# A graph kernel with groups of 64 nodes in place of 128, and rows of g spread to edges in three bf16 parts

## What is computed

```python
h = relu(layernorm(x))
x = x + gcn(h)          # D^-1/2 A D^-1/2 h W, relu; rows of edges' dst are summed into src
h = relu(layernorm(x))
msg_fwd  = concat(h[src], edge_attr) @ W_fwd  + b_fwd     # summed into dst
msg_back = concat(h[dst], edge_attr) @ W_back + b_back    # summed into src
x = x + layernorm(leaky(mean of the messages) + h)
```

## Time and profile before

| | us |
|---|---|
| median of 3 runs (4393.7 to 4401.2) | 4395.8 |
| the profiled execution | 4403.9 |
| its span | 4402.1 |
| POOL busy (69% of the span) | 3040.5 |
| PE busy (77%) | 3390.4 |
| DVE busy (72%) | 3169.3 |
| ACT busy (42%) | 1843.2 |

### The profile page before, as it was taken

One profiled execution on the slowest core, in us unless ns is written; L12 is line 12 of the kernel. 1 busy time (PEld: TensorE's weight loads), 2 busy tenths in 40 slices (PEclk: granted clock), 3 DMA queues, 4 the chain that ended last, 5 costly groups with the idle time before them and its releaser, 6 DMA issues. The chain is left out here.

```text
span 4402.1 us, 100368 instructions
## 1 busy us (share of the span) xinstructions
PE 3390.4 (77%) x30529; PEld 2833.3 (64%) x30529; DVE 3169.3 (72%) x8051; ACT 1843.2 (42%) x4498; POOL 3040.5 (69%) x1812
## 2 busy tenths in 40 slices
PE   1454599888889888889803499889888898889945
PEld 1344587777777777777703377767767677777635
DVE  6999888888888888878614776666666666666427
ACT  1021355545555555555404144444444444444513
POOL 2666488888888888888820688778777777777210
PEclk9989899999999999999956599999999999999977
DMA  9991587777777777777786555455445555554861
GB/s 162 279 217 16 128 142 140 139 140 135 135 141 139 141 136 135 137 135 141 129 131 120 105 84 85 75 78 82 77 77 78 84 77 80 77 83 72 97 124 30
DMA packets 682054, 504.19 MB, mean 115 GB/s; under 512 B 308854, under 2 KB 593920, under 8 KB 679754
## 3 DMA queue, kind: packets, MB, share of 16 engines
q0 software_dynamic: 260032, 176.60, 36.6%
q1 hardware_dynamic: 421475, 320.75, 29.9%
HBM read 283.43 MB, written 240.12 MB: 119 GB/s over the span
## 5 line engine op out<-in xcount | busy, mean ns | idle before, releaser
L1643 POOL DMA_INDIRECT gcn_sums<-shared,ds_to_i x752 | 1309.1, 1741 | 542.5 <-ACT shared L1895 327.6
L813 POOL DMA_INDIRECT gcn_sums<-fl_sums,fl_to_i x864 | 1459.3, 1689 | 290.9 <-DMA gcn_sums<-fl_sums,fl_to_i 151.9
L1850 PE MATMUL bank<-ds_counts,ds_parts 128*128 128x256 bf16 x3675 | 605.5, 278 | 0.0
L1039 ACT COPY fl_sums<-bank 128x256 f32<-128x256 f32 x864 | 324.7, 376 | 641.8 <-DMA gcn_sums<-fl_sums,fl_to_i 303.6
L1919 ACT COPY ds_turned<-bank 128x1024 bf16<-128x1024 bf16 (+1 forms) x325 | 313.1, 963 | 613.4 <-PE bank L1835 520.7
L1883 ACT CAST ds_counts<-bank 128x392 bf16<-128x392 f32 x800 | 382.9, 490 | 225.9 <-PE bank L1794 206.4
L1870 PE MATMUL bank<-ds_turned,ds_now 128*128 128x512 bf16 (+1 forms) x1950 | 463.7, 375 | 0.0
L851 DVE SCALAR_TENSOR_TENSOR fl_same<-fl_key_b,fl_pat,from_me 128x128 f32<-128x128 bf16 x864 | 375.5, 447 | 117.0 <-PE bank L967 93.1
L1779 DVE TENSOR_TENSOR src_sums<-src_sums,bank 128x512 f32<-128x512 f32 (+1 forms) x325 | 213.2, 656 | 278.8 <-PE bank L1870 274.2
L966 PE MATMUL bank<-fl_pay,fl_same 128*128 128x128 f32 x1728 | 350.9, 285 | 66.7 <-issue 38.1
L1812 PE MATMUL bank<-shared 128*128 128x128 f32 x1504 | 306.8, 308 | 115.1 <-DVE attr_sums L1696 87.1
(11 more groups left out here) (254 smaller groups left out, 7101.6 us busy)
## 6 DMA issues: line engine op xcount, KB each, us to landing
fl_attrs<-in_edge_attr SPq DMA_DIRECT2D x108, 512.0 KB
shared<-in_edge_attr SPq DMA_DIRECT2D x186, 256.0 KB
fl_rel_b<-dst_offset SPq DMA_DIRECT2D x108, 256.0 KB
fl_key_b<-src_key SPq DMA_DIRECT2D x108, 256.0 KB
gcn_sums<-zeros SPq DMA_DIRECT2D x40, 640.0 KB
shared<-src_key SPq DMA_DIRECT2D x94, 256.0 KB
gcn_sums<-fl_sums,fl_to_i POOLq DMA_INDIRECT x864
near<-src_float SPq DMA_DIRECT2D x1, 12892.0 KB
```

The costliest lines, as they stand in the source:

```text
L813: nc.gpsimd.indirect_dma_start(out=d.tab_gcn[j % K], out_offset=bass.IndirectOffsetOnAxis(ap=to_i[:, (GPI * kk + gi) % 4, j:j + 1], axis=0 ...
L1039: nc.scalar.copy(sums[:, h, j, :], sum_bank[j % 2][:, 0:2 * F]).then_inc(staged, 1)
L1643: nc.gpsimd.indirect_dma_start(out=d.tab_gcn[j % K].rearrange("n (two f) -> (n two) f", two=2), out_offset=bass.IndirectOffsetOnAxis(ap=to ...
L1850: ins = nc.tensor.matmul(row_bank[:, 0:2 * P], parts[:, tile, s, :], counts[:, h, tile, :, :].rearrange("p b q -> p (b q)"), start=(tile = ...
```

## The change

The window has W = 64 nodes in place of 128, in both stages. `sum_hot` halves, and so do the moving side of the window sums and the addition to `attr_sums`. In `first_layer` the 64 rows of g are loaded twice, onto both halves of the partitions. They are cut into three bf16 parts that add up to the f32 value: `top` (both halves at first), then `rest` = window - top, then the upper half of `top` is overwritten by bf16(rest), `mid` is the same on the lower half, and `low` = rest - mid. `spread_hot` becomes bf16, with `part_w` counting 0 to 63 on both halves, so one product over 128 partitions adds top and mid, and a second over 64 partitions adds low. ACT makes top and mid at chunks 1 and 3 of the group before, DVE rest and low at the same chunks. The diff, cut to its core:

```diff
+W = 64
-                nc.vector.tensor_scalar(wide[:, 0:1], wide[:, 0:1], P - 0.5, None, ALU.is_gt)
+                nc.vector.tensor_scalar(wide[:, 0:1], wide[:, 0:1], W - 0.5, None, ALU.is_gt)
...
-        spread_hot = sb("spread_hot", [P, J, P])
+        spread_hot = sb("spread_hot", [P, J, P], BF16)
+        part_w = sb("part_w", [P, 1])
+        top = sb("top", [P, 2, F], BF16)
+        low = sb("low", [W, 2, F], BF16)
+        rest = sb("rest", [P, F])
+        mid = sb("mid", [W, F], BF16)
-        sum_hot = sb("sum_hot", [P, J, P])
+        sum_hot = sb("sum_hot", [P, J, W])
...
-                    sp.dma_start(window[:, h, :], d.g[bass.ds(base, P), :]).then_inc(window_in[h], 16)
+                    for cut in (slice(0, W), slice(W, P)):
+                        sp.dma_start(window[cut, h, :], d.g[bass.ds(base, W), :]).then_inc(window_in[h], 16)
...
-                nc.vector.tensor_tensor(sum_hot[:], d.iota[:].unsqueeze(1).to_broadcast([P, J, P]), rec[:, h, 2, :].unsqueeze(2).to_broadcast([P, J, P]),
+                nc.vector.tensor_tensor(sum_hot[:], d.iota[:, 0:W].unsqueeze(1).to_broadcast([P, J, W]), rec[:, h, 2, :].unsqueeze(2).to_broadcast([P, J, W]),
...
-                at = bass.ds(base, P)
-                nc.vector.tensor_tensor(d.attr_sums[:, at], d.attr_sums[:, at], win_bank[:, 0:P], ALU.add).then_inc(window_added, 1)
+                at = bass.ds(base, W)
+                nc.vector.tensor_tensor(d.attr_sums[:, at], d.attr_sums[:, at], win_bank[:, 0:W], ALU.add).then_inc(window_added, 1)
+            def window_rest(i, kk, gi):
+                g, h = group(i, kk, gi), gi % 2
+                dve.wait_ge(top_ready, 3 * g + 1)
+                dve.wait_ge(window_in[h], 32 * loads(i, kk, gi))
+                nc.vector.tensor_tensor(rest[:], window[:, h, :], top[:, h, :], ALU.subtract).then_inc(rest_ready, 1)
+            def window_low(i, kk, gi):
+                g, h = group(i, kk, gi), gi % 2
+                dve.wait_ge(top_ready, 3 * g + 3)
+                dve.wait_ge(rest_ready, g + 1)
+                at_least(dve, row_ready, 2 * (g - 1))
+                nc.vector.tensor_tensor(low[:, h, :], rest[0:W, :], mid[:], ALU.subtract).then_inc(low_ready, 1)
...
-                    nc.vector.tensor_scalar(spread_hot[:], rel_b[:, h, :, :].rearrange("p q j -> p j q"), d.part[:, 0:1], None,
+                    nc.vector.tensor_scalar(spread_hot[:], rel_b[:, h, :, :].rearrange("p q j -> p j q"), part_w[:, 0:1], None,
                                             ALU.is_equal).then_inc(spread_ready, 1)
+                if j == 1:
+                    window_rest(i, kk, gi)
+                if j == 3:
+                    window_low(i, kk, gi)
...
                 if half == 0:
-                    pe.wait_ge(window_in[h], 16 * loads(i, kk, gi))
+                    pe.wait_ge(top_ready, 3 * g + 3)
+                    pe.wait_ge(low_ready, g + 1)
...
-                    last = nc.tensor.matmul(row_bank[:, q * F:(q + 1) * F], spread_hot[:, half * U + q, :], window[:, h, :], start=True, stop=True)
+                    here, hot = row_bank[:, q * F:(q + 1) * F], spread_hot[:, half * U + q, :]
+                    nc.tensor.matmul(here, hot, top[:, h, :], start=True, stop=False)
+                    last = nc.tensor.matmul(here, hot[0:W, :], low[:, h, :], start=False, stop=True)
...
-                    nc.tensor.matmul(win_bank[:, 0:P], attrs[:, h, jj, :], sum_hot[:, jj, :], start=(jj == 0), stop=(jj == J - 1))
+                    nc.tensor.matmul(win_bank[:, 0:W], attrs[:, h, jj, :], sum_hot[:, jj, :], start=(jj == 0), stop=(jj == J - 1))
...
+            def window_top(i, kk, gi):
+                g, h = group(i, kk, gi), gi % 2
+                act.wait_ge(window_in[h], 32 * loads(i, kk, gi))
+                at_least(act, row_ready, 2 * (g - 1))
+                nc.scalar.copy(top[:, h, :], window[:, h, :]).then_inc(top_ready, 1)
+            def window_mid(i, kk, gi):
+                g, h = group(i, kk, gi), gi % 2
+                act.wait_ge(rest_ready, g + 1)
+                at_least(act, low_ready, g)
+                nc.scalar.copy(top[W:P, h, :], rest[W:P, :]).then_inc(top_ready, 1)
+                nc.scalar.copy(mid[:], rest[0:W, :]).then_inc(top_ready, 1)
...
                     gi, j = divmod(c, J)
+                    if j == 1 and not (last and gi == GPI - 1):
+                        window_top(i, kk, gi + 1)
+                    if j == 3 and not (last and gi == GPI - 1):
+                        window_mid(i, kk, gi + 1)
                     keep_sums(i, kk, gi, j, first)
```

More of the change, by code:

```diff
@@ L739, in first_layer @@
         window_added = sem("window_added")
+        top_ready, rest_ready, low_ready = sem("top_ready"), sem("rest_ready"), sem("low_ready")
         added = [sem(f"added{k}") for k in range(K)]
@@ L901, in _ @@
             nc.vector.tensor_copy(numbers[:], d.iota[:]).then_inc(numbers_ready, 1)
-            dve.wait_ge(numbers_ready, 1)
+            nc.vector.tensor_copy(part_w[0:W, :], d.part[0:W, 0:1]).then_inc(numbers_ready, 1)
+            nc.vector.tensor_scalar(part_w[W:P, :], d.part[W:P, 0:1], float(W), None, ALU.subtract).then_inc(numbers_ready, 1)
+            dve.wait_ge(numbers_ready, 3)
             dve.wait_ge(gcn_zeroed, 1)
@@ L1053, in keep_pairs @@
                 nc.scalar.copy(to, pair_bank[n % 2][:, 0:PB * HH].rearrange("p (c k) -> p k c", c=PB)).then_inc(pair_copied, 1)
+            window_top(0, 0, 0)
+            window_mid(0, 0, 0)
             make_pay(0, 0, 0, 0)
@@ L1502, in dense_sums @@
         same = shared(J * P).rearrange("p (j q) -> p j q", j=J)
-        sum_hot = shared(J * P).rearrange("p (j q) -> p j q", j=J)
+        sum_hot = shared(J * W).rearrange("p (j q) -> p j q", j=J)
         sums = shared(4 * U * F).rearrange("p (u j f) -> p u j f", u=4, j=U)
@@ L1686, in spot_sums @@
                 at_least(dve, chunk_done, J * q)
-                nc.vector.tensor_tensor(sum_hot, d.iota[:].unsqueeze(1).to_broadcast([P, J, P]), rec[:, p, 2, :].unsqueeze(2).to_broadcast([P, J, P]),
+                nc.vector.tensor_tensor(sum_hot, d.iota[:, 0:W].unsqueeze(1).to_broadcast([P, J, W]), rec[:, p, 2, :].unsqueeze(2).to_broadcast([P, J, W]),
                                         ALU.is_equal).then_inc(sum_ready, 1)
@@ L1694, in add_window @@
                 at_least(dve, window_added, q)
-                here = bass.ds(base, P)
-                nc.vector.tensor_tensor(d.attr_sums[:, here], d.attr_sums[:, here], win_bank[:, 0:P], ALU.add).then_inc(window_added, 1)
+                here = bass.ds(base, W)
+                nc.vector.tensor_tensor(d.attr_sums[:, here], d.attr_sums[:, here], win_bank[:, 0:W], ALU.add).then_inc(window_added, 1)
             def prepare(i, h, gi, j, ahead):
@@ L1811, in sum_chunk @@
                 for jj in (range(3) if j == 2 else range(j, j + 1) if j > 2 else ()):
-                    nc.tensor.matmul(win_bank[:, 0:P], attrs[:, jj // U, jj % U, :], sum_hot[:, jj, :], start=(jj == 0), stop=(jj == J - 1))
+                    nc.tensor.matmul(win_bank[:, 0:W], attrs[:, jj // U, jj % U, :], sum_hot[:, jj, :], start=(jj == 0), stop=(jj == J - 1))
                 pe.wait_ge(same_ready, ch + 1)
```

## The result

The changed kernel takes 4452.1 us (median of 4 runs, 4444.9 to 4461.9), against 4394.8 for the kernel before on the same chip: ratio 1.0131 [1.0108, 1.0153]. The prediction was 4359 and faster; it is 57 us slower.

A forecast was written before the change was run, and what follows sets the result against it. GpSimd's scatters were taken to bound the first layer, GpSimd and TensorE together the second. First layer -17 us and second layer -20 us took 4395.8 to 4359 us, forecast range 4323 to 4387, with 80% from 4323 to 4394.

The forecast's parts named there:

- the term for the exact parts: First layer: VectorE's two new subtractions, 0.28 us each, stretch GpSimd's scatters by 3 us in all.
- The square law: Scatter stretches beside a VectorE instruction scale with its length squared; for sum one-hots (0.68/1.22)^2 = 0.31.
- (b): Rival: first-layer hand-offs between engines line up in series, 17.1 us a group against 16.1; slower, 4484 us; chance 0.09.
- Sum one-hots in the first layer: VectorE's one-hots, 1024 to 512 columns, stretch scatters less: GpSimd gets back 21 us, bounds 0 and 30.
- rival (a): Nothing to measure: stretches move to VectorE's next instruction, TensorE and GpSimd give back the second layer's gain; 4391 us, chance 0.12.
- The -45: The fastest end of the first layer's forecast, -17 us with a range of -45 to 0.
- Second layer: TensorE gains 22 us from narrow sums, GpSimd 28; stage forecast -20 us, range -28 to -8.
- the stage takes the smaller: Second layer: two engines share the bound, so of TensorE's 22 us and GpSimd's 28 the smaller counts, rounded to 20.
- (c): Rival: VectorE's spread one-hots get quicker with bf16 output, 30 us more gained; 4329 us, chance 0.06.
- (d): Rival: f32 loads are not the pace, 64 columns halve TensorE's window sums; second layer -102 us, 4277 us, chance 0.05.
- Spreading in bf16: First layer, TensorE: 16 f32 passes a group become 16 bf16 ones, 88 us less TensorE time, no gain in kernel time.
- the new waits: First layer: waits among ScalarE, VectorE and TensorE for window and parts, covered by slack and TensorE's saving; 1 us at stage start.

The follow-up runs named there:

- e6: The changed kernel with mid and low worked out on all 128 partitions instead of 64: 4359.8 us, ratio 0.9918 to before.
- e2: The changed kernel with only the bf16 parts, its sum one-hots, window sums and additions back at 128 columns: 4541.4 us, ratio 1.0341 to before.
- e1: The kernel before with W = 64 in the sums alone, g spread in f32 as before: 4360.1 us, ratio 0.9924 to before.
- e4: The changed kernel with VectorE waiting for the end of its own low before going on: 4343.1 us, ratio 0.9888 to before.
- e13: The changed kernel with low and mid over 128 partitions and VectorE waiting for its own low: 4346.3 us, ratio 0.9879 to before.
- e8: The changed kernel without the subtraction for low, its products and the waits for it: 4363.9 us, ratio 0.9918 to before.
- e10: The narrow sums alone plus one unused VectorE subtraction a group over partitions 0 to 63, where low would stand: 4513.1 us, ratio 1.0252 to before.
- e14: The narrow sums alone plus one unused VectorE subtraction a group over all 128 partitions, where low would stand: 4402.1 us, ratio 1.0002 to before.

## Why the prediction was wrong

- **The step that failed** is the term for the exact parts: "VectorE: two subtractions, 0.28 us each by L836 ... Their own stretches: 2 x (0.28/1.22)^2 x 30 = 3 us". Size, number and duration were right (278 ns), and one of the two, low over 64 partitions, cost some 100 us (first layer 1836.2 us, and 1736.1 with the same subtraction over 128 in e6). The row I priced it from, L836, is over 128, as is every VectorE row that I used. The square law has a stretch end with the instruction that causes it; here it ends at VectorE's next pause or addition out of PSUM at the latest, up to 6 us on. The diff shows `rest[0:W, :]`, a form without a row among mine, and I took one value for it instead of a bound. A bound was to be had: the longest run of VectorE in before without a pause or an addition out of PSUM, 5.9 us, once in each of 27 slots, 160 us. e2 came to that: its 72 scatters of over 2.6 us hold 164 us.
- **The wrong rival.** (b) was the only slower one. Its price (4484) came near, its mechanism didn't: GpSimd never waited for ScalarE.
- **Sum one-hots in the first layer**: -21 predicted. Their own stretches fell much as the square law says (29.6 to 13.5 in e1, 0.46; predicted 0.31), but e1's layer is 3 us longer. The stretches beside other instructions grew by as much, which is rival (a)'s mechanism. With the long scatters gone the first layer gains 10 us (e4), 8 (e13) or 5 (e6), for -17; that is within what profiled executions differ by. The -45 at the end of this layer's range is worked out nowhere.
- **Second layer**: -20 (-28 to -8) predicted, -49 measured in the two profiles. Over all profiles it is less sure: the fifteen with the narrow sums alike average 1602.6 us, the two with the wide ones 1641.8 and 1627.3, so some 32. TensorE's wait for the added window was right: 69.7 us from 87.1 (predicted 68). The excess fell from 136 to 93 us, 43 and not 28. The step "the stage takes the smaller" gave too little; that the stage gained GpSimd's share instead of TensorE's is a guess.

```profile
PE bank L1863 <- DVE attr_sums L1747: 69.7, 27, 9.5
```

- **L879 with bf16 output** 1.16 us (predicted 1.17), so no (c). **The f32 loads** of L1863 still start 0.11 us apart at 64 columns, so no (d):

```profile
3022.34 0.30 PEld L1863 LDWEIGHTS bank<-shared 128*128 128x128 f32 x2
```

- **Spreading in bf16**: "16 bf16 ones", 0.06 us apart, 88 us of TensorE's time gone. It went the other way. The eight f32 loads of a half stood 0.11 us apart, and the loads of top and low, which take turns, stand 0.16 apart, so a half lasts some 0.4 us longer:

```profile
1022.08 0.09 PEld L981 LDWEIGHTS bank<-fl_low,fl_spread_hot 64*128 64x128 bf16 x1
1022.24 0.10 PEld L980 LDWEIGHTS bank<-fl_top,fl_spread_hot 128*128 128x128 bf16 x1
1022.40 0.09 PEld L981 LDWEIGHTS bank<-fl_low,fl_spread_hot 64*128 64x128 bf16 x1
```

Without low's products (e8) top's loads do stand 0.06 apart. The prediction priced them from L998's row and took its loads for 98 columns, where the row says 128x128. It was right that this is off the path: e8 is no faster than e6. But the 0.9 us a group that it set against the new waits were not there.

The Trainium skill (SBUF — State Buffer, Who interferes with whom) says that VectorE and GpSimd share a port pair under an exclusive lock, which whoever issues first holds for the whole instruction. It also says that a VectorE instruction with at most one SBUF input, outside the 2-port modes, leaves GpSimd alone. The traces agree that one keeps the other out (a scatter of 5.25 us at 1001.10), and that an addition out of PSUM lets a held scatter in (40 of 56 in e10). They differ in how long: from low at 999.96 VectorE ran through ten further instructions before the scatter got in. They differ on one input as well: beside L856, which reads one tensor, the prediction's own pairing has 46 us of stretches, and its 1.17 us for 1024 values, against L827's 1.22 with two inputs, shows no faster mode, so its "agree with it" holds for L827 alone. That the cause of the long scatters is this lock is inferred; no run here shows the lock itself.

With the mend the kernel is faster by about what was expected: 1.2% or 53 us by the ratio in e13 (46 by the medians), 0.8% or 36 us in e6, where -37 was forecast. That the sum comes out so well is partly luck: the first layer gave less than forecast and the second more.

## What to carry to other kernels

Look at the maximum beside the median of a line: a mean that rises with an unmoved median is a few very long instances, and what they share is a place. Before a small VectorE instruction is added beside GpSimd's scatters, look at which partitions it covers and how long VectorE then runs without a pause; write it over all 128 partitions (e6 costs no more than leaving low out, e8; the idle one of e14 did cost 0.8%), or put a wait for its own result behind it (e4). And price a new form from a row of that form, or give it a bound that is as long as the run it stands in.

## What the runs showed of the hardware that was not expected

- A VectorE instruction of 0.28 us over partitions 0 to 63 or 0 to 95, in a run without pauses, holds most indirect scatters that begin up to some 1.2 us behind its start (30 of 36, 56 of 67, 61 of 71), and a few that begin up to 2.0 us behind it (5 in the changed kernel, 9 in e10). They get in at VectorE's first pause or addition out of PSUM at the latest, from which they still take 1.4 us; 0.05 us of pause are enough (1004.90 to 1004.95). The longest took 6.97 us (e10). Over 0 to 127 or 64 to 127 it doesn't. Whether partition 127, the last 32 or others decide was not tried.
- With one input in place of two the effect is there in part (17 long scatters for 30).
- Two bf16 products that take turns, over 128 and over 64 rows, into the same bank start 0.16 us apart; those over 128 rows alone start 0.06 apart (e8).
- In the changed kernel TensorE's granted clock was 0.92 from 1000 to 1400 us and 0.99 before: both near the 2.4 GHz level. It is lower where the long scatters are (0.97 in e1, 0.93 in e10; 0.96 in e6), but not only there (0.94 in e4, which has none). A clock of 0.94 alone does not make them, then.

```profile
1000.00:1400.00 400.00, 363.95 (x3034) 289.87 (x3035) 306.67 (x922) 209.78 (x609) 340.02 (x188) 0.92 0.73 129
```
